# A linear-attention head whose seven levels are run on TensorE in two stretches in place of three

## The chip, the cores and the metric

One core of one Trainium2 chip runs the whole kernel. The metric is the device time in microseconds of one execution. A profiled execution leaves a trace, in which times are counted from the first instruction.

## The reference, cut to what matters

A decoder block of 16 sequences of 128 rows and 256 features: gated linear attention with 8 heads, then cross-attention, then a mixture of experts that takes 2 of 8. The change lies in the first part:

```python
q = l2norm(x @ Wq); k = l2norm(x @ Wk); v = x @ Wv; alpha = sigmoid(x @ Wg)   # per head: 128 wide
S_t = alpha_t[:, None] * S_{t-1} + k_t[:, None] * v_t[None, :]                 # scan over 128 steps
o_t = S_t.T @ q_t
out = concat_heads(o) @ Wo
```

## The kernel before

**Tiling.** The 16 sequences are 4 groups of 4. A group has 4 x 128 = 512 columns, and the unit of work is one head of one group: 32 units, counted n = 0 to 31, with h = n % 8 the head and i = n // 8 the group. Each engine has one list of instructions in an order written out by hand, and waits on counting semaphores. There is no loop on the chip.

**The levels.** The scan is replaced by a sum over pairs (s, t) of one sequence. A pair belongs to level l when s and t lie in neighbouring halves of a block of 2^(l+1) steps; s = t is the diagonal. For each level the operands q and k have to carry the product of the alphas from the middle of the block. So level l's operands are made from level l-1's: VectorE multiplies one half of them by spans of alpha (`decay(n, l)`, L646, for l = 6 L653), ScalarE copies the other half (`carry(n, l)`, L438), and neither may begin before both parts of level l-1 are there. Each level has one buffer, which unit n+1 may write only when TensorE has read it for unit n. TensorE multiplies the operands of a level in tiles of 32 x 32 (`block_products`, L1053, levels 0 to 4 and the diagonal; L1083, levels 5 and 6) into two banks, `lo_bank` and `hi_bank`. VectorE takes what a mask owns of the diagonal and levels 0 to 4 into `blocks` (`keep`, L677), six per unit. ScalarE spreads `blocks` over the diagonal of `attnT` (`expand_blocks`, L460) and copies levels 5 and 6 into it (`expand_wide`, L450 and L452).

**The order on TensorE** in iteration n: parts of the later layers at place "S", `project_v(n)` (L1043), alpha's projection for n+1 (L1030, `wg_sb`), the first run of levels, q's projection for n+1 (`wq_sb`), `attend_transposed(n-2)` (L1116), k's projection for n+2 (`wk_sb`), the second run of levels, `output_projection(n-2)` (L1128), parts at place "A", `attend(n-1)` (L1109), parts at "B", the third run of levels, and `norms(n)` (L1100). Results of projections go round a ring of four banks: a projection waits until the bank filled four fills before has been read.

**The order on ScalarE** in iteration n: `expand_wide(n-1)`, which waits for the last run of levels and for the norms of n-1; carries; `alpha_out(n+1)` (L403); `expand_blocks(n-1)`; `q_out(n+1)` (L410, L412); `oT_out(n-2)` (L465), for which `output_projection(n-2)` waits; `k_out(n+2)` (L419, L421); carries of n+1; copies for the later layers. Parts of the later layers stand before `alpha_out` ("early": `gelu` at h = 0, the exponentials of `probs_out` at h = 3, copies of `rowsT` at h = 5) and after `expand_blocks` ("mid": `gate_exp_out` at h = 6). When the function changes, a table is loaded.

**The order on VectorE** in iteration n: `norm_floor(n-1)` (L686), which waits for `expand_wide(n-1)`; the two keeps of `hi_bank` of n-1; decays; `v_scaled(n)` (L695), which frees the bank that k's projection takes; parts of later layers; `span_products(n+1)` (L663); `q_decayed(n+1)` (L704); the four keeps of `lo_bank` of n; decays of n+1; `o_scaled(n-1)` (L710).

Of the kernel before, what the change touches and what calls it, by code (L numbers as in the profile page):

```python
# [18 lines left out]
LEVELS = 7  # L19
BLOCK = 32  # L20
OUTER = LEVELS - 1
INNER = 5
# [15 lines left out]
def decoder_kernel(nc, x, ctx, ctxT, wq, wk, wv, wg, wo, xwT, gateT, expert, up_b,  # L38
# [7 lines left out]
    U = NG * H  # L46
# [5 lines left out]
    with ExitStack() as stack:  # L52
# [85 lines left out]
        lo_bank, hi_bank, acc0, acc1 = (bank(n) for n in ("lo_bank", "hi_bank", "acc0", "acc1"))  # L138
# [137 lines left out]
            return view(tensor, first, [[second - first, 2], [2 * w, N // (2 * w)], [1, w]])  # L276


        RUNS = ((0, 2), (1, 3, 4), (5, 6))
        DONE = {l: j + 1 for j, l in enumerate(l for run in RUNS for l in run)}  # L280
        LO_KEPT = 4

# [115 lines left out]
        def _(act):  # L398
# [24 lines left out]
            def carry(n, l):  # L423

                if n > 0:
                    act.wait_ge(level_mm, LEVELS * (n - 1) + DONE[l])
                if l == 1:
                    act.wait_ge(q0_set, n + 1)
                    act.wait_ge(k_set, n + 1)
                else:  # L430
                    act.wait_ge(decayed, OUTER * n + l - 1)
                    act.wait_ge(carry_set, OUTER * n + l - 1)
                if l < OUTER:
                    src, dst = (halves(n, m, 2 ** (l - 1), False) for m in (l - 1, l))
                else:
                    src, dst = (view(states, m * 2 * N + T // 2, [[N - BLOCK, 2], [T, GB], [1, BLOCK]])
                                for m in (l - 2, l - 1))
                nc.scalar.copy(dst, src).then_inc(carry_set, 1)  # L438

            def expand_wide(n):  # L440
                act.wait_ge(level_mm, LEVELS * (n + 1))
                act.wait_ge(norm_mm, min(n + 3, U + 1))
                positive(act, o_mm, n)
                near = hi_bank[:, AT_NEAR:AT_FAR].rearrange("p (b t) -> p b t", b=GB // 2)
                far = hi_bank[:, AT_FAR:AT_NORM].rearrange("p (b t) -> p b t", b=GB // 2)
                by_parity = attnT[:].rearrange("p (b m) t -> p b m t", m=2)
                for m in range(2):
                    for lo in (0, 2 * BLOCK):
                        at = lo + BLOCK * m
                        nc.scalar.copy(by_parity[lo:lo + BLOCK, :, m, lo + BLOCK:lo + 2 * BLOCK], near[at:at + BLOCK])  # L450
                    at = T // 2 * m
                    last = nc.scalar.copy(by_parity[0:T // 2, :, m, T // 2:T], far[at:at + T // 2])  # L452
                last.then_inc(near_out, 1)
# [83 lines left out]
            alpha_out(0)  # L537
            split_weights(3)
            q_out(0)
            for l in range(1, INNER):  # L540
                carry(0, l)
            for n in range(U):
                if n >= 1:
                    expand_wide(n - 1)
                carry(n, 5)
                carry(n, 6)
                tail_part(n, "early")
                if n + 1 < U:
                    alpha_out(n + 1)
                if n >= 1:  # L550
                    expand_blocks(n - 1)
                tail_part(n, "mid")
                if n + 1 < U:
                    q_out(n + 1)
                if n >= 2:
                    oT_out(n - 2)
                if n + 2 < U:
                    k_out(n + 2)
                if n + 1 < U:
                    for l in range(1, INNER):  # L560
                        carry(n + 1, l)
                tail_part(n, "end")
            expand_wide(U - 1)
# [39 lines left out]
        def _(dve):  # L603
# [60 lines left out]
                                            view(src, off + 1, [[2, m]]), ALU.mult).then_inc(span_set, 1)  # L664


            KEPT = ((lo_bank, 0, 0), (lo_bank, 1, 1), (lo_bank, 2, 3), (lo_bank, 3, 5), (hi_bank, 0, 2), (hi_bank, 1, 4))

            def keep(n, k):
                of_bank, at, mask = KEPT[k]  # L670
                positive(dve, kept, KEEPS * n + k)
                if k == 0:
                    dve.wait_ge(level_mm, LEVELS * n + INNER)
                    positive(dve, attnT_set, n)
                if k == LO_KEPT:
                    dve.wait_ge(near_out, n + 1)
                nc.vector.copy_predicated(blocks[:].rearrange("p b t -> p (b t)"), owned[:, mask].bitcast(U32),  # L677
                                          of_bank[:, N_IN * at:N_IN * at + N_IN]).then_inc(kept, 1)
# [211 lines left out]
            q_decayed(0)  # L890
            norm_floor(-1)
            dve.wait_ge(c_in, N_C)
            for l in range(1, INNER):
                decay(0, l)
            for n in range(U):
                if n >= 1:
                    norm_floor(n - 1)
                    for k in range(LO_KEPT, KEEPS):
                        keep(n - 1, k)
                decay(n, 5)  # L900
                decay(n, 6)
                v_scaled(n)
                tail_part(n, "early")
                if n + 1 < U:
                    span_products(n + 1)
                    q_decayed(n + 1)
                tail_part(n, "late")
                for k in range(LO_KEPT):
                    keep(n, k)
                if n + 1 < U:  # L910
                    for l in range(1, INNER):
                        decay(n + 1, l)
                tail_part(n, "mid")
                if n >= 1:
                    o_scaled(n - 1)
                if n == 0:
                    dve.wait_ge(w_in, N_W)
                tail_part(n, "end")
# [88 lines left out]
        def _(pe):  # L1007
# [49 lines left out]
            def levels(n, run):  # L1057

                if run == RUNS[0]:
                    pe.wait_ge(q_set, n + 1)  # L1060
                    pe.wait_ge(q0_set, n + 1)
                    pe.wait_ge(k_set, n + 1)
                    positive(pe, kept, KEEPS * (n - 1) + LO_KEPT)
                    block_products(lo_bank, 0, state0[:, 2 + n % 3], q_raw[:, n % 2])
                if run == RUNS[1]:
                    positive(pe, kept, KEEPS * n)
                    pe.wait_ge(norm_sq_set, n + 2)
                for l in run:
                    if l > 0:
                        pe.wait_ge(decayed, OUTER * n + l)  # L1070
                        pe.wait_ge(carry_set, OUTER * n + l)
                    tensor, at_q, at_k = state_at(n, l)
                    q, k = view(tensor, at_q, [[1, N]]), view(tensor, at_k, [[1, N]])
                    if l < INNER:
                        last = block_products(*((hi_bank, l // 2) if l % 2 else (lo_bank, 1 + l // 2)), k, q)
                    else:
                        w = 2 ** l
                        for b in range(GB):
                            m, col = b % 2, (AT_NEAR if l == INNER else AT_FAR) + w * (b // 2)
                            for s in (0, 2 * BLOCK) if l == INNER else (0, BLOCK):  # L1080
                                row = s + (BLOCK if l == INNER else 2 * BLOCK) * m
                                start = T * b + (s + w if l == INNER else w)
                                last = mm(hi_bank[row:row + BLOCK, col:col + w], k[:, T * b + s:T * b + s + BLOCK],  # L1083
                                          q[:, start:start + w], start=True, stop=True)
                    last.then_inc(level_mm, 1)
# [164 lines left out]
            for n in range(U + 1):  # L1250
                tail_part(n, "S")
                if n < U:
                    project_v(n)
                if n + 1 < U:
                    project(wg_sb, ("g", n + 1)).then_inc(g_mm, 1)
                if n < U:
                    levels(n, RUNS[0])
                if n + 1 < U:
                    project(wq_sb, ("q", n + 1)).then_inc(q_mm, 1)
                if n >= 2:  # L1260
                    attend_transposed(n - 2)
                if n + 2 < U:
                    project(wk_sb, ("k", n + 2)).then_inc(k_mm, 1)
                if n < U:
                    levels(n, RUNS[1])
                if n >= 2:
                    output_projection(n - 2)
                if n < U:
                    tail_part(n, "A")
                if n >= 1:  # L1270
                    attend(n - 1)
                tail_part(n, "B")
                if n < U:
                    levels(n, RUNS[2])
                if n + 1 < U:
                    norms(n)
            attend_transposed(U - 1)
# [84 lines left out]
```

## Time and profile before

| | |
|---|---|
| median of 3 runs | 564.17 us (562.89 to 567.42) |
| the profiled execution | 563.17 us, its span 561.4 us |
| granted clock of TensorE, mean | 0.951 of full speed |
| busy: TensorE, VectorE, ScalarE | 488.9, 383.1, 356.9 us |
| the 32 units | from 27.7 us to about 500 us of the span |

The span is the time from the first to the last instruction; 1.8 us of the profiled execution lie outside it. Busy times are sums over the instructions of an engine. The units repeat, so one unit can be read row by row and the others by how they differ from it.

### The profile page before, as it was taken

How to read it: one execution, taken by the hardware profiler on the slowest of the kernel's cores; microseconds unless marked ns; L12 is line 12 of the kernel's file. 1: busy time of each engine (PE TensorE's matmuls, PEld its weight loads, DVE VectorE, ACT ScalarE, POOL GpSimd, SP SyncE). 2: the span in 40 equal slices, each digit the busy share in tenths (PEclk: the TensorE clock that was granted, in tenths of full speed). 3: DMA queues.
4: the chain of work that ended last, by engine and by line, in shares of the span. 5: the costliest groups of instructions: out<-in, count | busy, mean ns of one | idle time of the engine just before them, and what ended most of it. 6: DMA issues, size and time to landing. Idle time of an engine off the chain costs nothing. (4 is left out here: it accounts for less than half of the span.)

```text
span 561.4 us, 25935 instructions
## 1 busy us (share of the span) xinstructions
PE 488.9 (87%) x11232; PEld 407.4 (73%) x11232; DVE 383.1 (68%) x1069; ACT 356.9 (64%) x825; POOL 85.1 (15%) x71
## 2 busy tenths in 40 slices
PE   1798999999988999899988999899988999775616
PEld 1587888888877888787867888688867887664415
DVE  4588887766786888765686887765775888614541
ACT  4667787766758677567758677577748676442202
POOL 1012111111111111410111111410111111300020
PEclk9999999999999999899999999899989999997557
DMA  8800000001010100210010100210000100201021
GB/s 334 252 3 5 4 4 4 4 4 40 4 41 2 41 4 4 77 41 22 23 40 5 40 4 4 78 40 22 23 2 4 40 5 4 78 0 39 0 75 37
DMA packets 15264, 20.35 MB, mean 36 GB/s; under 512 B 1200, under 2 KB 12976, under 8 KB 15152
## 3 DMA queue, kind: packets, MB, share of 16 engines
q1 hardware_dynamic: 13872, 14.49, 7.6%
q0 software_dynamic: 1280, 4.20, 2.6%
q8 instruction: 89, 1.46, 1.1%
q14 instruction: 23, 0.19, 0.1%
HBM read 16.60 MB, written 2.10 MB: 33 GB/s over the span
## 5 line engine op out<-in xcount | busy, mean ns | idle before, releaser
L438 ACT COPY states<-states 128x512 f32<-128x512 f32 (+1 forms) x160 | 94.6, 592 | 95.3 <-DVE states L646 88.6
L363 POOL TENSOR_TENSOR rnorm<-norm_sq,neg_half 128x8 f32<-128x8 f32 (+1 forms) x33 | 53.8, 1631 | 291.0 <-DVE norm_sq L686 291.0
L646 DVE TENSOR_TENSOR states<-states,spans 128x512 f32<-128x512 f32 x128 | 88.5, 691 | 12.2 <-DVE states L646 4.6
L1128 PE MATMUL acc<-wo_sb,oT_sb 128*128 128x256 f32 x256 | 63.8, 392 | 8.2 <-ACT oT_sb L465 8.2
L1030 PE MATMUL ring<-xnT,wk_sb 128*128 128x512 f32 x192 | 55.7, 429 | 8.9 <-DVE v_sb L695 6.0
L1043 PE MATMUL ring<-wv_sb,xnT 128*128 128x256 f32 x384 | 57.5, 302 | 0.6 <-DVE wv_sb L877 0.6
L1128 PEld LDWEIGHTS acc<-wo_sb,oT_sb 128*128 128x128 f32 x256 | 46.0, 189 | 15.3 <-ACT oT_sb L465 9.3
L1030 PE MATMUL ring<-xnT,wq_sb 128*128 128x512 f32 x192 | 53.1, 412 | 1.7 <-ACT rowsT L469 1.0
L677 DVE COPY_PREDICATED blocks<-owned,lo_bank 128x128 f32<-128x128 uint32 x128 | 38.5, 301 | 20.2 <-PE lo_bank L1053 14.8
L1043 PEld LDWEIGHTS ring<-wv_sb,xnT 128*128 128x128 f32 x384 | 50.9, 200 | 1.1 <-DVE wv_sb L877 0.7
L1030 PE MATMUL ring<-xnT,wg_sb 128*128 128x512 f32 x192 | 51.0, 402 | 0.0
L1030 PEld LDWEIGHTS ring<-xnT,wk_sb 128*128 128x128 f32 x192 | 36.1, 200 | 16.8 <-DVE v_sb L695 7.1
L1030 PEld LDWEIGHTS ring<-xnT,wq_sb 128*128 128x128 f32 x192 | 33.6, 188 | 9.2 <-ACT rowsT L469 1.4
L1030 PEld LDWEIGHTS ring<-xnT,wg_sb 128*128 128x128 f32 x192 | 35.0, 195 | 6.2 <-DVE xnT L749 0.2
L460 ACT COPY attnT<-blocks 32x128 f32<-32x128 f32 x128 | 37.4, 292 | 1.1
L1109 PEld LDWEIGHTS ring<-v_sb,attnT 128*128 128x128 f32 x256 | 33.0, 192 | 5.2 <-issue 4.3
L450 ACT COPY attnT<-hi_bank 32x64 f32<-32x64 f32 x128 | 26.0, 203 | 16.0 <-PE hi_bank L1100 8.5
L1109 PE MATMUL ring<-v_sb,attnT 128*128 128x128 f32 x256 | 33.8, 275 | 0.4 <-issue 0.4
L1100 PE MATMUL hi_bank<-ones,squares 128*32 128x1 f32 x2048 | 26.7, 173 | 7.8 <-issue 5.9
L1100 PEld LDWEIGHTS hi_bank<-ones,squares 128*32 128x32 f32 x2048 | 24.2, 110 | 10.1 <-issue 7.9
L663 DVE TENSOR_TENSOR spans<-spans 128x128 f32<-128x128 f32 (+3 forms) x128 | 28.4, 222 | 4.4
L1053 PE MATMUL lo_bank<-states 128*32 128x32 f32 x2048 | 29.6, 198 | 1.5 <-issue 1.5
(145 smaller groups left out, 852.4 us busy)
## 6 DMA issues: line engine op xcount, KB each, us to landing
x_buf<-x_dram SPq DMA_DIRECT2D x4, 512.0 KB, 4.2
ctxT_sb<-ctxT_dram SPq DMA_DIRECT2D x8, 256.0 KB, 3.4
ctx_sb<-ctx_dram SPq DMA_DIRECT2D x4, 512.0 KB, 4.8
out_dram<-x_mid SPq DMA_DIRECT2D x8, 256.0 KB, 2.1
states<-wk_dram SPq DMA_DIRECT2D x1, 1024.0 KB, 6.1
states<-wg_dram SPq DMA_DIRECT2D x1, 1024.0 KB, 8.1
states<-wq_dram SPq DMA_DIRECT2D x1, 1024.0 KB, 10.1
v_sb<-wv_dram SPq DMA_DIRECT2D x1, 1024.0 KB, 11.7
```

The source lines that it names most:

```text
L363: nc.gpsimd.tensor_tensor(rnorm[:, m % 4, first:last], norm_sq[:, first:last], neg_half[:, first:last], ALU.pow).then_inc(rnorm_set, 1)
L438: nc.scalar.copy(dst, src).then_inc(carry_set, 1)
L460: last = nc.scalar.copy(attnT[lo:lo + BLOCK, :, lo:lo + BLOCK], blocks[lo:lo + BLOCK])
L646: nc.vector.tensor_tensor(dst, src, by, ALU.mult).then_inc(decayed, 1)
L663: nc.vector.tensor_tensor(spans[:, span_at(l):span_at(l) + m], view(src, off, [[2, m]]), view(src, off + 1, [[2, m]]), ALU.mult).then_inc( ...
L677: nc.vector.copy_predicated(blocks[:].rearrange("p b t -> p (b t)"), owned[:, mask].bitcast(U32), of_bank[:, N_IN * at:N_IN * at + N_IN]). ...
L1030: last = mm(dst[:], w[:, a, c, P * h:P * h + P], xnT[:, i % 2, b, c], start=(c == 0 and k == 0), stop=(c == KC - 1 and k == 2))
L1043: last = mm(dst[:, 2 * P * k:2 * P * k + 2 * P], xnT[:, i % 2, a, c, T * b:T * b + T], wv_sb[:, w, c, 2 * P * pair:2 * P * pair + 2 * P], ...
L1053: last = mm(dst[BLOCK * r:BLOCK * r + BLOCK, to:to + BLOCK], left[:, at:at + BLOCK], right[:, at:at + BLOCK], start=True, stop=True)
L1100: last = mm(hi_bank[BLOCK * r:BLOCK * r + BLOCK, to:to + 1], squares[:, a, at:at + BLOCK], ones[:], start=True, stop=True)
L1109: last = mm(dst[:, P * b:P * b + P], attnT[:, b], v_sb[:, n // 2 % 2, b, n % 2], start=True, stop=True)
L1128: last = mm(accs[z][:, D * m:D * m + D], oT_sb[:, n % 2, T * b:T * b + T], wo_sb[:, h], start=(h == 0 and m == 0), stop=(h == H - 1 and m ...
```

## The change

Levels 1, 3 and 4 no longer have a run of their own between k's projection and the output projection. Level 1 joins the first run, levels 3 and 4 the last one. With that the banks are dealt anew: the diagonal and levels 0 to 2 lie in `lo_bank`, levels 3 to 6 and the norms in `hi_bank`, and the masks of the keeps follow. The four keeps of `lo_bank` wait for level 2 in place of level 4. The carries and decays of levels 3 and 4, whose buffers TensorE now frees only at the end of an iteration, move on ScalarE and VectorE from the end of iteration n to iteration n+1: behind `expand_wide` on ScalarE, in front of `v_scaled` on VectorE, while the decays of levels 5 and 6 go behind `v_scaled`. No instruction is added or taken away.

```diff
--- before.py
+++ after.py
@@ -276,7 +276,8 @@
             return view(tensor, first, [[second - first, 2], [2 * w, N // (2 * w)], [1, w]])
 
 
-        RUNS = ((0, 2), (1, 3, 4), (5, 6))
+        RUNS = ((0, 1, 2), (3, 4, 5, 6))
+        EARLY = 2
         DONE = {l: j + 1 for j, l in enumerate(l for run in RUNS for l in run)}
         LO_KEPT = 4
 
@@ -537,11 +538,13 @@
             alpha_out(0)
             split_weights(3)
             q_out(0)
-            for l in range(1, INNER):
+            for l in range(1, EARLY + 1):
                 carry(0, l)
             for n in range(U):
                 if n >= 1:
                     expand_wide(n - 1)
+                carry(n, 3)
+                carry(n, 4)
                 carry(n, 5)
                 carry(n, 6)
                 tail_part(n, "early")
@@ -557,7 +560,7 @@
                 if n + 2 < U:
                     k_out(n + 2)
                 if n + 1 < U:
-                    for l in range(1, INNER):
+                    for l in range(1, EARLY + 1):
                         carry(n + 1, l)
                 tail_part(n, "end")
             expand_wide(U - 1)
@@ -664,13 +667,13 @@
                                             view(src, off + 1, [[2, m]]), ALU.mult).then_inc(span_set, 1)
 
 
-            KEPT = ((lo_bank, 0, 0), (lo_bank, 1, 1), (lo_bank, 2, 3), (lo_bank, 3, 5), (hi_bank, 0, 2), (hi_bank, 1, 4))
+            KEPT = ((lo_bank, 0, 0), (lo_bank, 1, 1), (lo_bank, 2, 2), (lo_bank, 3, 3), (hi_bank, 0, 4), (hi_bank, 1, 5))
 
             def keep(n, k):
                 of_bank, at, mask = KEPT[k]
                 positive(dve, kept, KEEPS * n + k)
                 if k == 0:
-                    dve.wait_ge(level_mm, LEVELS * n + INNER)
+                    dve.wait_ge(level_mm, LEVELS * n + DONE[2])
                     positive(dve, attnT_set, n)
                 if k == LO_KEPT:
                     dve.wait_ge(near_out, n + 1)
@@ -890,16 +893,18 @@
             q_decayed(0)
             norm_floor(-1)
             dve.wait_ge(c_in, N_C)
-            for l in range(1, INNER):
+            for l in range(1, EARLY + 1):
                 decay(0, l)
             for n in range(U):
                 if n >= 1:
                     norm_floor(n - 1)
                     for k in range(LO_KEPT, KEEPS):
                         keep(n - 1, k)
+                decay(n, 3)
+                decay(n, 4)
+                v_scaled(n)
                 decay(n, 5)
                 decay(n, 6)
-                v_scaled(n)
                 tail_part(n, "early")
                 if n + 1 < U:
                     span_products(n + 1)
@@ -908,7 +913,7 @@
                 for k in range(LO_KEPT):
                     keep(n, k)
                 if n + 1 < U:
-                    for l in range(1, INNER):
+                    for l in range(1, EARLY + 1):
                         decay(n + 1, l)
                 tail_part(n, "mid")
                 if n >= 1:
@@ -1072,7 +1077,7 @@
                     tensor, at_q, at_k = state_at(n, l)
                     q, k = view(tensor, at_q, [[1, N]]), view(tensor, at_k, [[1, N]])
                     if l < INNER:
-                        last = block_products(*((hi_bank, l // 2) if l % 2 else (lo_bank, 1 + l // 2)), k, q)
+                        last = block_products(*((lo_bank, 1 + l) if l < 3 else (hi_bank, l - 3)), k, q)
                     else:
                         w = 2 ** l
                         for b in range(GB):
@@ -1261,8 +1266,6 @@
                     attend_transposed(n - 2)
                 if n + 2 < U:
                     project(wk_sb, ("k", n + 2)).then_inc(k_mm, 1)
-                if n < U:
-                    levels(n, RUNS[1])
                 if n >= 2:
                     output_projection(n - 2)
                 if n < U:
@@ -1271,7 +1274,7 @@
                     attend(n - 1)
                 tail_part(n, "B")
                 if n < U:
-                    levels(n, RUNS[2])
+                    levels(n, RUNS[1])
                 if n + 1 < U:
                     norms(n)
             attend_transposed(U - 1)
```

## Rows read from the trace of the kernel before

**Rows 1.** The page, busy time by engine, share of the span, instructions.

```profile
PE 488.9 (87%) x11232; PEld 407.4 (73%) x11232; DVE 383.1 (68%) x1069; ACT 356.9 (64%) x825; POOL 85.1 (15%) x71
```

**Rows 2.** Waits of all engines: total us, times, longest us.

```profile
PEld hi_bank L1053 <- issue: 11.7, 32, 0.6
...
PE acc L1128 <- ACT oT_sb L465: 8.2, 8, 2.9
...
PE ring L1030 <- DVE v_sb L695: 6.0, 3, 2.0
```

**Rows 3.** TensorE's timeline of unit 17 and first of 18: start, us, operation.

```profile
266.80 1.69 PE L1043 MATMUL ring<-wv_sb,xnT 128*128 128x256 f32 x12
...
270.42 0.46 PE L1053 MATMUL lo_bank<-states 128*32 128x32 f32 x32
270.80 1.66 PE L1030 MATMUL ring<-xnT,wq_sb 128*128 128x512 f32 x6
272.30 0.60 PE L1116 MATMUL ring<-ident,o_sb 128*128 128x128 f32 x4
272.66 1.65 PE L1030 MATMUL ring<-xnT,wk_sb 128*128 128x512 f32 x6
274.23 0.76 PE L1053 MATMUL hi_bank<-states 128*32 128x32 f32 x64
...
275.23 1.99 PE L1128 MATMUL acc<-wo_sb,oT_sb 128*128 128x256 f32 x8
...
279.17 1.69 PE L1043 MATMUL ring<-wv_sb,xnT 128*128 128x256 f32 x12
```

**Rows 4.** ScalarE's timeline of unit 17.

```profile
266.98 0.42 ACT L450 COPY attnT<-hi_bank 32x64 f32<-32x64 f32 x2 [3.48 <-PE hi_bank L1100]
...
268.28 0.62 ACT L438 COPY states<-states 128x512 f32<-128x512 f32 x1
269.88 0.41 ACT L438 COPY states<-states 128x256 f32<-128x256 f32 x1 [0.98 <-DVE states L646]
270.31 0.60 ACT L403 ACTIVATE alpha<-ring 128x512 f32<-128x512 f32 x1
270.81 1.21 ACT L460 COPY attnT<-blocks 32x128 f32<-32x128 f32 x4
272.50 0.59 ACT L410 COPY q_raw<-ring 128x512 f32<-128x512 f32 x1 [0.48 <-PE ring L1030]
...
273.48 0.59 ACT L465 COPY oT_sb<-ring 128x512 f32<-128x512 f32 x1
```

**Rows 5.** VectorE's timeline of unit 17, its decays and v.

```profile
269.12 0.68 DVE L646 TENSOR_TENSOR states<-states,spans 128x512 f32<-128x512 f32 x1
269.90 0.49 DVE L653 TENSOR_TENSOR states<-states,spans 128x128 f32<-128x128 f32 x2
270.31 0.68 DVE L695 TENSOR_TENSOR v_sb<-ring,rnorm 128x512 f32<-128x512 f32 x1
```

**Rows 6.** TensorE's timeline, output projection in unit 19.

```profile
306.93 2.00 PE L1128 MATMUL acc<-wo_sb,oT_sb 128*128 128x256 f32 x8 [0.92 <-ACT oT_sb L465]
```

**Rows 7.** Windows, units 18 to 24: length, busy PE PEld DVE ACT POOL, clock, DMA.

```profile
279.17:294.57 15.40, 13.43 (x353) 11.33 (x346) 13.55 (x39) 9.48 (x23) 2.69 (x2) 1.00 0.12 37
294.57:312.11 17.54, 15.51 (x373) 13.53 (x366) 12.86 (x40) 14.16 (x36) 2.69 (x2) 1.00 0.01 4
312.11:327.02 14.91, 14.34 (x353) 11.95 (x347) 13.52 (x42) 9.15 (x23) 2.75 (x2) 1.00 0.12 39
327.02:340.95 13.93, 13.51 (x354) 11.48 (x347) 11.03 (x27) 10.76 (x27) 1.64 (x1) 1.00 0.01 4
340.95:358.10 17.15, 15.38 (x349) 12.25 (x347) 13.73 (x55) 11.30 (x26) 6.12 (x5) 1.00 0.18 50
358.10:374.48 16.38, 16.38 (x355) 13.41 (x351) 10.21 (x24) 12.02 (x26) 1.67 (x1) 0.90 0.15 44
374.48:392.38 17.90, 17.60 (x378) 15.14 (x370) 10.25 (x24) 12.82 (x28) 1.64 (x1) 1.00 0.08 24
```

## The prediction

> **What bounds the kernel now.** I read the page's busy times first: TensorE is busy for 87% of the span, the others for 68% and less [rows 1]. Then the waits, for what takes the rest: inside the 32 units hardly anything but 8.2 us for `oT_sb` (8 times) and 6.0 us for `v_sb` (3 times) [rows 2]. So TensorE's own list sets the pace of a unit. Then the timelines of one plain unit, to see how far behind the other engines' chain of waits is. Unit 17 begins at B = 266.80 and unit 18 at 279.17: 12.37 us without a gap [rows 3]. ScalarE begins `expand_wide` at 266.98, B + 0.18, as early as it can, since it had waited [rows 4]. Its order then runs: carry 5, a wait of 0.98 us for VectorE, carry 6 at 269.88, alpha at 270.31, `expand_blocks`, q at 272.50, oT at 273.48, which ends at 274.07. The output projection that needs oT begins at 275.23. The cover is 1.16 us, and the bound in a plain unit is TensorE only for as long as that cover lasts. This is the number to watch.
>
> **The work on TensorE.** The same instructions remain. Run 2 takes 274.23 to 275.23, 1.00 us for three levels; the last level of run 1 takes 270.42 to 270.80, 0.38 us [rows 3]. So level 1 in the first run costs 0.36 and levels 3 and 4 in the last one 0.64, together the 1.00 that goes. What remains is the entry into a run: from k's projection to the tiles is 1.57 us (272.66 to 274.23), from q's to the full transposes 1.50 us (270.80 to 272.30) [rows 3]. I take 0.07 us a unit, 2.2 us in all. The weight path shows more at that entry: 11.7 us of idle, 32 times, 0.37 us each [rows 2]; the matmuls cover most of it, so 0.37 is the upper bound. Entering the longer runs elsewhere is no new cost, as those runs were there. The Trainium skill ("TensorE: Matmul & The Clock Gate", The mechanism) says that a weight load overlaps matmuls in flight only where their row groups differ, so that tiles cannot be loaded ahead behind a full-array matmul. The idle weight path at the entry fits that; it would make a removed entry worth the whole 0.37, the first rival below.
>
> **When TensorE wants oT.** Before at B + 8.43 (275.23 less 266.80). Now 1.00 and 0.07 go from in front of it and 0.36 comes in: B + 7.72, which is 0.71 earlier.
>
> **When ScalarE has oT.** Carries 3 and 4 now stand between `expand_wide` and carry 5, and each waits for VectorE's part of the level below. Counted from E, the start of `expand_wide`, with unit 17's durations [rows 4, 5]: carry 3 starts at E + 1.30 (268.28 less 266.98). VectorE starts its first decay at E + 2.14, behind the norms and two keeps as before, and ends it at 2.82. Carry 4 follows at 2.90. Decay 4 starts 0.78 behind decay 3, as decay 6 behind decay 5 now, at 2.92, and ends at 3.60. Carry 5 starts at 3.68. But decay 5 stands behind `v_scaled`, which begins near 3.5 and takes 0.68 less some overlap, so decay 5 runs from 4.16 to 4.84. Carry 6 starts at E + 4.90, where before it was 2.90 (269.88). ScalarE is 2.0 us later. From carry 6 the rest has no more room: 0.43 to alpha, 0.50 to `expand_blocks`, 1.21 to q, whose own result is ready by then, so that the 0.48 us of waiting there goes, 0.98 to oT, 0.59 for oT. That is E + 8.61, B + 8.79. In unit 19, where oT is late already, the output projection starts at 306.93 [rows 6]; I add 0.05 for the step over the semaphore: B + 8.84. Bounds on the delay: 1.4 if `v_scaled` were to cost the chain nothing, 2.2 if each handshake costs 0.1 more.
>
> TensorE wants it at 7.72. It waits for 1.12 us, with attention, the last levels and the norms queued behind that wait, and the next `expand_wide` behind these. So nothing catches it up. The remainder of the unit was 3.94 (275.23 to 279.17) and is 4.58 with 0.64 of levels 3 and 4. A plain unit takes 8.84 + 4.58 = 13.42, against 12.37: 1.05 more. I take 1.0, since other plain units lag by some tenths at their start now, which the emptier end of ScalarE's iteration takes away. Plain are units 2 to 8, 9, 17 and 25: 10 of them, **+10.0**.
>
> **The other units**, from unit 18 to 24's windows, in which length less busy time is the wait [rows 7]. The heads repeat for three groups.
> - h = 2 (18): 15.40 long, 1.97 idle for `v_sb`. VectorE enters this unit late, behind the residual and the norm's statistics. Now it keeps `lo_bank` without waiting for a second run, and has two decays of 0.68 fewer in front of them, so that wait goes. 13.42 and the transposes of x2T (15.40 less 1.97 less 12.37, 1.06) make 14.5: -0.9, three times **-2.8**.
> - h = 3 (19): 17.54 long, 2.03 idle, of which 0.92 is for oT [rows 6]. It starts at B + 12.36. The exponentials stand in the same chain, where the table load covers part of the 2.0; I take the start as B + 12.95, less the late start of ScalarE that goes. With 0.64 behind: +1.2, **+3.7**.
> - h = 4 (20): 14.91 long, 0.57 idle. Cross-attention in front of v gives ScalarE some 2 us. No wait for oT; the 0.5 at the start goes: **-1.6**.
> - h = 5 (21): 13.93 long. Copies of `rowsT` stand behind carry 6, and q's projection waits for their bank (0.42 now). That wait grows by the 2.0 less what the transposes in front cover: +1.5, **+4.6**.
> - h = 6 (22): a table load and `gate_exp` stand in the chain, 1.4 us. oT at B + 8.8 + 1.4 = 10.2, against 8.9 now (8.43 and some 0.5 for the gate's matmuls in front, an estimate), and 0.64: +2.0 twice, and +2.5 in unit 30, which has no k projection in front: **+6.5**.
> - h = 7 (23, clock 0.90): a table load of 1.3 stands before alpha. The slow clock covers it in part: +0.8 twice; unit 31 has neither g nor q nor k in front, +2.0: **+3.6**.
> - h = 0 with experts (24): 0.30 idle, all of it for oT. ScalarE is 2.0 later, 0.64 behind it: +2.65 twice, **+5.3**.
>
> The sum is 10.0 - 2.8 + 3.7 - 1.6 + 4.6 + 6.5 + 3.6 + 5.3 = 29.3 us. On the profiled execution's 563.17 that is 592.5 (1.8 of them outside the span). The median of the runs is 1.0 above that execution, inside their spread, so I leave **592.5 us**.
>
> **The rivals.**
> - *TensorE keeps its pace.* The point from which it decides: the cover of 1.16 less the 0.71 by which TensorE is earlier, 0.45 us. If ScalarE's chain grows by less, oT never stalls, and what moved is hidden. For it: TensorE has no gap in unit 17, and ScalarE's last carries were late at the end of an iteration before. Against it: the two carries stand in front of alpha in an ordered queue, and growing by 2.0 is four times the limit. It gives 2.2 for the entries, 5.9 for the waits for `v_sb` [rows 2] and 1.6 for h = 4: 563.2 - 9.7 = 553.5. With an entry worth 0.37, 11.7 in place of 2.2, it is 544. Without either relief, 561. By the skill's rule on row groups it would be the 544.
> - *Half of it.* Only the units in which oT is late already, or has a table load in its chain, lose, and the plain ones fit: the above less the plain ones' 10.0 is 582; with the lower bound of the chain (1.4 in place of 2.0 in some 27 units, 16 us less) 576.
> - *The clock.* Unit 23 shows a mean granted clock of 0.90, so part of it ran at the lower of the two levels, 1.2 GHz [rows 7]. The new waits of over 3 us at h = 0 and h = 3 and of over 2 us at h = 6 might bring more such stretches. Unit 23 has no wait and would last some 14.6 at full speed (a plain unit, keys and the transposes, an estimate), so one costs 1.5 to 2; six of them 9 to 12: 601 to 604.
>
> **How the numbers follow.** My forecast, a stall of about 1 us in each unit, has 0.65, with its own range of 583 to 600. Half of it 0.16, the clock 0.08, TensorE keeps its pace 0.11. What leaves out no more than 2 in 10 is 572 to 602: the forecast, most of the half case and some of the clock. One per cent, 5.6 us, is about what a measurement tells from no change. Faster by more than that takes the rival with its reliefs: 0.07. Within it: that rival without the reliefs, or both effects small: 0.06. Slower 0.87.
>
> **What would show it.** In the trace after: waits of the output projection for `oT_sb` in some 25 units in place of 8, and 30 us in place of 8; plain units 13.4 us long; carry 6 4.9 us behind the start of `expand_wide`, ScalarE waiting 2 us at the end of an iteration for the norms; no more waits for `v_sb`; the run of levels 3 to 6 without a wait in front. If plain units last 12.3 us with oT on time, the step "when ScalarE has oT" is wrong. It would be wrong too if VectorE's chain were faster than its rows, or if `expand_wide` could start before B.

## The result

The changed kernel takes 612.85 us (median of 4 runs, 609.35 to 613.44) against 563.53 us: a ratio of 1.085 (95% interval 1.078 to 1.092). The profiled execution has a span of 610.8 us, 49.4 more than before. Of all executions below one (of e1, 575.87 us) was in a slower state of the chip; the ratios leave it out, the median of e1 has it in.

The page of the changed kernel, busy times and the granted clock of TensorE by slices:

```profile
PE 504.7 (83%) x11232; PEld 419.1 (69%) x11232; DVE 380.4 (62%) x1069; ACT 358.9 (59%) x825; POOL 83.5 (14%) x71
...
PEclk9999899999989999999998999998989998788656
```

Against [rows 1]: TensorE executes the same 11232 matmuls but is busy for 15.8 us more, and the rest of its span has grown from 72.5 us (561.4 less 488.9) to 106.1 (610.8 less 504.7), 33.6 us more. Together these are the 49.4. A busy time that grows with the same instructions is the clock: the mean granted clock fell from 0.951 to 0.927. In windows of 1 us the lower level appears in 4 stretches (13.6 us in all) before the last unit begins in the kernel before, and in 11 (35.5 us) in the changed one.

The waits of TensorE in the changed kernel: total us, times, longest. They answer to [rows 2], and the last line is one more of the kernel before.

```profile
PE acc L1133 <- ACT oT_sb L466: 35.2, 22, 3.2
...
PE hi_bank L1105 <- issue: 6.5, 4, 2.2
...
PE ring L1048 <- issue: 4.2, 4, 1.3
PE ring L1035 <- issue: 3.2, 4, 1.7
PE hi_bank L1058 <- issue: 3.1, 8, 0.5
...
PE lo_bank L1058 <- issue: 2.2, 3, 0.8
```

```profile
PE hi_bank L1100 <- issue: 5.9, 13, 0.5
```

Waits for oT went from 8.2 us to 35.2. TensorE's waits for `v_sb` (6.0) have no row any more. Waits on issue, in which TensorE waits for nothing that the profile shows, grew from 12.7 us to 20.7. They are not new: the last line, of the kernel before, is as large as the one for `v_sb`, and I passed over it.

Two kinds are mixed in them. In units 14, 22 and 30 TensorE stops several times in a row for 0.2 to 0.5 us, always while the rows of the experts' weights are being fetched (a transfer of some 6 us, 227.9 to 233.8 us in unit 14 of the kernel before). These come to 5.1 us before, 3.1 in the changed kernel, 5.1 in e5, 3.1 in e6 and 5.4 in e7 below, and to nothing in the other runs, which fetch the same rows. What ties them to the transfer is not shown. The rest is 7.5 us before and 17.5 in the changed kernel; the long stops in it are of the kind that unit 2 shows below.

TensorE's timeline of the plain unit 5, to be laid beside [rows 3]:

```profile
94.56 1.69 PE L1048 MATMUL ring<-wv_sb,xnT 128*128 128x256 f32 x12
...
98.17 0.75 PE L1058 MATMUL lo_bank<-states 128*32 128x32 f32 x64
...
100.70 1.65 PE L1035 MATMUL ring<-xnT,wk_sb 128*128 128x512 f32 x6
103.37 1.99 PE L1133 MATMUL acc<-wo_sb,oT_sb 128*128 128x256 f32 x8 [1.03 <-ACT oT_sb L466]
...
106.19 0.77 PE L1058 MATMUL hi_bank<-states 128*32 128x32 f32 x64
...
107.19 0.76 PE L1105 MATMUL hi_bank<-ones,squares 128*32 128x1 f32 x64
107.89 1.70 PE L1048 MATMUL ring<-wv_sb,xnT 128*128 128x256 f32 x12
```

Its unit is 13.33 us long (94.56 to 107.89). The output projection starts at B + 8.81 with 1.03 us of waiting. ScalarE in the same unit, beside [rows 4]:

```profile
94.74 0.42 ACT L451 COPY attnT<-hi_bank 32x64 f32<-32x64 f32 x2 [2.62 <-PE hi_bank L1105]
...
96.03 0.62 ACT L439 COPY states<-states 128x512 f32<-128x512 f32 x1
97.63 0.62 ACT L439 COPY states<-states 128x512 f32<-128x512 f32 x1 [0.97 <-DVE states L649]
98.41 0.62 ACT L439 COPY states<-states 128x512 f32<-128x512 f32 x1 [0.16 <-DVE states L649]
99.61 0.41 ACT L439 COPY states<-states 128x256 f32<-128x256 f32 x1 [0.58 <-DVE states L649]
100.04 0.60 ACT L404 ACTIVATE alpha<-ring 128x512 f32<-128x512 f32 x1
...
101.76 0.58 ACT L411 COPY q_raw<-ring 128x512 f32<-128x512 f32 x1
...
102.73 0.59 ACT L466 COPY oT_sb<-ring 128x512 f32<-128x512 f32 x1
```

`expand_wide` begins at E = 94.74, carry 3 at E + 1.29, carry 4 at 2.89, carry 5 at 3.67, carry 6 at 4.87, alpha at 5.30, oT at 7.99 and ends at 8.58. Carries 4, 5 and 6 each wait for VectorE.

The second loss stands in unit 2, the same work, 15.68 us long. TensorE's timeline:

```profile
59.22 2.00 PE L1133 MATMUL acc<-wo_sb,oT_sb 128*128 128x256 f32 x8 [1.01 <-ACT oT_sb L466]
...
62.04 0.76 PE L1058 MATMUL hi_bank<-states 128*32 128x32 f32 x64
...
63.05 0.68 PE L1105 MATMUL hi_bank<-ones,squares 128*32 128x1 f32 x54
65.90 0.26 PE L1105 MATMUL hi_bank<-ones,squares 128*32 128x1 f32 x10 [2.17 <-issue]
66.09 2.81 PE L1048 MATMUL ring<-wv_sb,xnT 128*128 128x256 f32 x12
68.70 1.99 PE L1035 MATMUL ring<-xnT,wg_sb 128*128 128x512 f32 x6
```

After 54 of the 64 matmuls of the norms TensorE stands for 2.17 us, though nothing releases it, and then goes on with the other 10. The transfers of 60 to 68 us in 40 slices of 0.2 us:

```profile
GB/s 0 0 0 0 0 0 0 0 0 0 0 0 0 0 0 0 82 0 0 0 0 0 0 0 0 0 0 0 0 0 0 0 0 0 0 0 0 0 0 82
...
q8 instruction: 2, 0.03, 1.9%
```

There is nothing but two packets of instructions of 16 KB. The first lies in the 17th slice, 63.2 to 63.4 us; TensorE, which has just taken 300 short instructions since 62.04 (150 matmuls and their weight loads), stops at about 63.7 and goes on at 65.90. Behind it the clock falls; the window from 64 to 70 us (length, busy PE PEld DVE ACT POOL, clock, DMA share, GB/s):

```profile
64.00:70.00 6.00, 4.10 (x26) 3.85 (x26) 2.83 (x13) 2.54 (x9) 2.64 (x2) 0.72 0.01 3
```

v and g's projection (66.09 to 70.62) take 4.53 us in place of 3.00 in unit 5.

The other stops look alike. Besides the rows of short stops there are 13 of 0.6 us or more within the units of the changed kernel. In 12 of them TensorE goes on 2.2 to 2.9 us after a packet of instructions has started (in one after 4.0). Count TensorE's matmuls and weight loads from the start: the stops stand at numbers 1447, 2201, 3207, 4965, 5217, 6975, 10485, 12743, 13993, 14745, 14997, 18511 and 21017. Each distance is a whole number of times 250 to 252, and 252 is the mean of a packet (22464 in 89 packets). That fits stops at the borders of packets; the profile shows how large packets are, but not which instructions are in one.

### The profile page after: what moved, and what is told of

The parts are those of the page before. It is cut to its first block and busy times, and to the rows that moved or that the text cites. A ratio compares the mean times of both kernels' runs of the same rounds, so it can differ in the third digit from the quotient of the medians.

```text
span 610.8 us, 25935 instructions
## 1 busy us (share of the span) xinstructions
PE 504.7 (83%) x11232; PEld 419.1 (69%) x11232; DVE 380.4 (62%) x1069; ACT 358.9 (59%) x825; POOL 83.5 (14%) x71
## 5 line engine op out<-in xcount | busy, mean ns | idle before, releaser
L1133 PE MATMUL acc<-wo_sb,oT_sb 128*128 128x256 f32 x256 | 71.3, 427 | 35.4 <-ACT oT_sb L466 35.2
L1133 PEld LDWEIGHTS acc<-wo_sb,oT_sb 128*128 128x128 f32 x256 | 50.8, 208 | 53.5 <-ACT oT_sb L466 46.6
L1048 PE MATMUL ring<-wv_sb,xnT 128*128 128x256 f32 x384 | 59.2, 307 | 4.8 <-issue 4.2
L1048 PEld LDWEIGHTS ring<-wv_sb,xnT 128*128 128x128 f32 x384 | 52.2, 204 | 5.7 <-issue 4.5
L689 DVE TENSOR_SCALAR norm_sq<-hi_bank 128x8 f32<-128x8 f32 (+1 forms) x33 | 5.5, 166 | 61.2 <-ACT attnT L453 44.0
L713 DVE TENSOR_TENSOR o_sb<-ring,rnorm 128x512 f32<-128x512 f32 x32 | 22.1, 690 | 33.4 <-PE ring L1114 33.2
L666 DVE TENSOR_TENSOR spans<-alpha 128x256 f32<-128x256 f32 x32 | 13.6, 424 | 37.0 <-ACT alpha L404 36.9
```

Source lines behind the costliest of these rows:

```text
L713: nc.vector.tensor_tensor(o_sb[:], ring_of(("o", n))[:].rearrange("p (b v) -> p b v", b=GB), rnorm[:, (n - 1) % 4, 0:GB].unsqueeze(2).broa ...
L1048: last = mm(dst[:, 2 * P * k:2 * P * k + 2 * P], xnT[:, i % 2, a, c, T * b:T * b + T], wv_sb[:, w, c, 2 * P * pair:2 * P * pair + 2 * P], ...
L1133: last = mm(accs[z][:, D * m:D * m + D], oT_sb[:, n % 2, T * b:T * b + T], wo_sb[:, h], start=(h == 0 and m == 0), stop=(h == H - 1 and m ...
```

## The experiments

I tested two theories. S: all of it is ScalarE's chain in front of oT, and the clock follows from its waits. F: the longer run of small tiles (levels 3 to 6 and the norms, 320 instructions in some 2 us) also outruns the supply of instructions. Each ratio is to the kernel before on the same chip. "Low clock" is the time at the lower level up to the last unit's start, from windows of 1 us.

| | ratio (95%) | TensorE busy, rest of span | oT | issue | low clock |
|---|---|---|---|---|---|
| before | 1 | 488.9, 72.5 | 8.2 | 12.7 | 13.6 |
| changed | 1.085 (1.078 to 1.092) | 504.7, 106.1 | 35.2 | 20.7 | 35.5 |
| e1 | 1.021 (1.013 to 1.029) | 494.1, 75.9 | 16.2 | 13.9 | 23.9 |
| e3 | 1.042 (1.040 to 1.044) | 488.5, 86.3 | 30.1 | 5.5 | 10.2 |
| e5 | 0.981 (0.977 to 0.985) | 485.9, 65.7 | 10.2 | 9.8 | 6.8 |

All columns but the ratio are of one execution each. From one execution of e1 to the next the mean granted clock went from 0.934 to 0.952, and one stretch at the lower level (3.4 us) is worth 0.003 of it (an estimate: half of 3.4 in 570). So a difference of a few stretches between two kernels says little.

**e1, carries 5 and 6 behind oT.** Two runs on TensorE as in the changed kernel.

```diff
 (ScalarE)                                   (VectorE)
   carry(n, 3); carry(n, 4)                    decay(n, 3); decay(n, 4); v_scaled(n); decay(n, 5)
-  carry(n, 5); carry(n, 6)                  - decay(n, 6)
   ... alpha_out, expand_blocks, q_out         ... span_products(n + 1), q_decayed(n + 1)
   oT_out(n - 2)                               keep(n, 0..3)
+  carry(n, 5); carry(n, 6)                  + decay(n, 6)
```

(The spans of level 5, which decay 6 reads, get a second place for odd n.)

> The changed kernel, with carries 5 and 6 moved on ScalarE from in front of alpha to behind oT (VectorE's decay 6 follows the four keeps). Theory S (ScalarE's chain in front of oT is the whole cause; the lower clock follows from its waits): the output projection stands at B + 7.7 to 7.9 in a plain unit, waits for oT fall from 35 us to under 8, low-clock stretches inside the units from 12 to about 4, time 556 to 568 us. Theory F (the longer run of small tiles, levels 3 to 6 and the norms, outruns the supply of instructions to TensorE): the waits for oT go as well, but TensorE's idle time put down to issue stays near 19 us, as do half of the low-clock stretches, time 575 to 590 us.

Measured 572.78 us, ratio 1.021 (1.013 to 1.029), between the two ranges. The waits in question:

```profile
PE acc L1134 <- ACT oT_sb L466: 16.2, 12, 3.2
...
PE hi_bank L1106 <- issue: 5.2, 6, 1.9
...
PE ring L1049 <- issue: 3.7, 3, 1.6
```

Plain units without a stop are 12.15 us long (5, 8, 17), 0.2 to 0.3 less than before, and their output projection stands at B + 7.65. So the theory on ScalarE's chain holds where it speaks, and the timing on TensorE's side (7.72) too. But units 2, 3, 7 and 9 are 14.2, 14.7, 15.4 and 14.1 us long (unit 3 has no stop of its own: the clock is low in it from 63.3 us on, behind that of unit 2), and the row of unit 2 is the one from above, at the same instruction:

```profile
62.49 0.26 PE L1106 MATMUL hi_bank<-ones,squares 128*32 128x1 f32 x10 [1.89 <-issue]
```

The numbers 2201, 6975, 10485, 13993, 18511 and 21017 are places of stops in e1, e2 and e4 as well. oT fell only to 16.2, as it stays late in the units with exponentials (B + 10.2) or experts.

**e2, two runs, carries and decays where they stood before.**

```diff
-        EARLY = 2
+        EARLY = 4
-   carry(n, 3..6)                                (ScalarE)
+   carry(n, 5); carry(n, 6)
-   decay(n, 3); decay(n, 4); v_scaled(n); decay(n, 5); decay(n, 6)
+   decay(n, 5); decay(n, 6); v_scaled(n)         (VectorE)
```

> Two runs on TensorE and the new banks as in the changed kernel, but all carries and decays stand where they stood before (levels 1 to 4 at the end of an iteration, where those of levels 3 and 4 now wait for the last run to have read their buffers). Theory S: oT comes at about B + 6.9, no waits for it in plain units, but the wait at the iteration's end makes VectorE late with v in units after residual and statistics: 558 to 572 us. Theory F: the same with 10 to 20 us more, from issue idle near 19 us and the low-clock stretches behind it: 575 to 590 us.

Measured 581.22 us, ratio 1.038 (1.032 to 1.044): oT 13.8 us, issue 22.1 us, low clock 34.1 us, as theory F had it. A second way to take the new carries away from in front of oT leaves the same stops, and units 2, 3, 7 and 9 as long (14.2, 14.7, 16.0 and 14.2 us).

**e3, levels 3 and 4 in a run of their own.** ScalarE and VectorE as changed.

```diff
-        RUNS = ((0, 1, 2), (3, 4, 5, 6))
+        RUNS = ((0, 1, 2), (3, 4), (5, 6))
+   levels(n, RUNS[1])          # (3, 4), between k's projection and
    output_projection(n - 2)
```

> The changed kernel, in which TensorE takes levels 3 and 4 in a run of their own between k's projection and the output projection; ScalarE and VectorE as in the changed kernel. Theory S: oT still comes at B + 8.8, but TensorE does 0.66 us of the work while it waits: plain units 12.7 us, 16 to 20 us less than the changed kernel's 613, so 592 to 597. Theory F: the run in front of v is short again, so that the issue idle falls from 19 us to about 11 and with it low-clock stretches: 578 to 590 us.

Measured 580.29 us, the waits:

```profile
PE acc L1133 <- ACT oT_sb L466: 30.1, 25, 2.9
...
PE hi_bank L1058 <- issue: 2.7, 1, 2.7
```

Plain units are 12.68 us, as both theories had it; their output projection is at B + 8.82 as before the edit, so the chain on ScalarE is untouched. But issue idle is 5.5 us (1.5 of it in the units), the low clock 10.2 us, and units 2, 3, 7 and 9 lose their extra (12.8, 13.6, 14.4, 12.7). The gain over the changed kernel is 4.3 points. The waits for oT are 0.25 to 0.45 us in plain units here and up to 2.7 elsewhere. Nine of those in the units are of 1.8 us or more; right behind two of them (2.02 us before 294.1, 1.85 before 393.0) the clock falls, and behind the other seven it doesn't.

**e4, v behind all decays.**

```diff
-                v_scaled(n)
                 decay(n, 5)
                 decay(n, 6)
+                v_scaled(n)
```

> The changed kernel with v_scaled moved on VectorE behind the decays of levels 5 and 6; nothing else. Theory S: carry 6 starts 0.65 us earlier behind the start of expand_wide (4.25 in place of 4.9), plain units shrink from 13.33 to 12.7 us, waits for oT from 35 to about 20 us, and with fewer low-clock stretches 588 to 598 us. Theory F: the waits for oT shrink as well but issue idle stays near 19 us with its low clock: 598 to 603 us.

Measured 596.05 us, ratio 1.070 (1.063 to 1.078). Plain units are 12.95 us (13.33 changed), a gain of 0.4 and not 0.65; oT 30.2, issue 18.8, low clock 17.1 us. The issue idle stays, as theory F had it. VectorE's order in front of carry 6 has its price, but is the smaller part of what a plain unit lost.

**e5, both cures: e1's edit and e3's together.** Banks and the first run as in the changed kernel.

> Both cures together: carries 5 and 6 behind oT as in e1, and levels 3 and 4 in a run of their own in front of the output projection as in e3; diagonal and levels 0 to 2 still in the first run, banks as in the changed kernel. If the 49 us are these two causes (S and F) and the low clock that follows their idle: waits for oT about 14 us as in e1 (heads with exponentials or experts), issue idle about 6 us as in e3, no waits for v, low-clock stretches in the units 3 to 5, time 548 to 560 us, same as before or faster. If the new banks or the longer first run carry a cost of their own, 565 us or more.

Measured 554.56 us, faster than the kernel before. The page's first line and TensorE's, and its waits:

```profile
span 551.6 us, 25935 instructions
...
PE 485.9 (88%) x11232; PEld 406.5 (74%) x11232; DVE 376.2 (68%) x1069; ACT 353.7 (64%) x825; POOL 84.1 (15%) x71
```

```profile
PE acc L1134 <- ACT oT_sb L466: 10.2, 8, 2.9
...
PE hi_bank L1106 <- issue: 5.1, 11, 0.5
```

No unit waits for v, and nothing remains of the 49 us. With e1, e3 and the changed kernel it makes a square: two runs in place of three cost 4.0 points with late carries (e1 against e5) and 4.3 with carries in front (changed against e3); carries in front cost 6.1 points with three runs (e3 against e5) and 6.4 with two (changed against e1). So the two causes add up, to within the intervals of about a point. e5 also shows that the new share of the banks and the longer first run cost nothing.

**e6, 128 instructions more at the start.** The changed kernel with 32 more calls, which the profile has as 64 matmuls and 64 weight loads:

```diff
             pe.wait_ge(ident_in, 16)
+            for _ in range(32):
+                mm(lo_bank[:, 0:BLOCK], ident[:], ident[:, 0:BLOCK], start=True, stop=True)
```

> The changed kernel with 32 extra small matmuls at the start of TensorE's list (128 instructions of it), where it waits for the first input anyway; nothing in the units changes. Theory F (instructions come in packets of a fixed count, and a packet is late when its border falls into the run of small tiles): the idle put down to issue moves to other units than 2, 3, 7 and 9 (15.68, 14.64, 16.29 and 15.58 us long in the changed kernel), which shrink to 13.4 to 14.5, while others grow; the time stays within 600 to 620 us. Theory S, or any cause that lies in the units' own work: the same units stay long.

Measured 621.28 us, ratio 1.097 (1.092 to 1.102), a little above the range. The first unit starts 7.7 us later (35.03 against 27.31), since the new matmuls hold TensorE from 5.03 to 18.89 us, and its next work started at 9.70 without them; from there to the last unit's start it takes 499.3 us, against 498.1. Within that the lengths moved: unit 2 from 15.68 to 14.35, 7 from 16.29 to 15.07, 9 from 15.58 to 14.32, 11 from 20.28 to 18.88, while 4 grew from 13.83 to 15.30, 12 from 13.62 to 15.99, 26 from 18.28 to 20.23 and 27 from 17.81 to 20.44. Unit 3 hardly changed (14.65 to 14.22). The stops stand on the same grid of numbers, with the 128 new instructions counted in: at 3711, 6727, 7229 and 9233, again 250 to 252 or a multiple apart, and at 12745, where the changed kernel has one at 12743, but 128 instructions earlier in the work. Work that is identical in each unit stalls by its place in TensorE's list: this is the supply of instructions, not the work. Unit 7 came down less than expected.

**e7, attention between levels 3 and 4 and levels 5 and 6.** As e1, but the last run is short.

```diff
+   levels(n, RUNS[1])          # (3, 4)
    attend(n - 1)
    tail_part(n, "B")
-   levels(n, RUNS[1])          # (3, 4, 5, 6)
+   levels(n, RUNS[2])          # (5, 6)
```

> As e1 (572.8 us, issue idle 13.9), but attention and the later layers' parts at place B stand between levels 3 and 4 and levels 5 and 6, so that the last run is again as short as before and the output projection starts as early as in e1. Theory F: the issue idle falls to 5 to 8 us and the low-clock stretches in the units from 8 to 3 to 5, time 553 to 562 us. If not the length of the run of small tiles but their place at the end of the unit matters: 570 to 575 us as e1.

Measured 576.59 us, ratio 1.018 (1.013 to 1.023), no better than e1: issue 14.5, low clock 20.1 us. Theory F had 553 to 562 us, so as I had written it, by the length of one run, it is wrong. Half of it came true: 5.4 of the 14.5 us are stops during the experts' fetches, which e1 has none of, so the other kind fell from 13.9 us to 9.1. The stop stands at the same instruction still, only shorter:

```profile
62.31 0.26 PE L1106 MATMUL hi_bank<-ones,squares 128*32 128x1 f32 x10 [1.05 <-issue]
```

Attention takes 1.0 us for 16 instructions (8 matmuls), so from levels 3 and 4 to the norms there are as many as before, and 16 more, in 3 us in place of 2. In e5 the output projection lies between as well, 1.8 us for another 16, and the stops in units 2, 3, 7 and 9 are gone. So an unbroken run is not needed; a count over some 3 us fits these runs, where the 3 us are my estimate. The stops of unit 2 also show what sets their length. TensorE goes on 2.4 us after the packet's start in e1 and 2.6 in e7, but 178 instructions remained to be taken at that start in e7 and 63 in e1. Why that packet starts so late is open.

**e8, the same results with fewer instructions.** As e1, with the norms by whole columns of weights:

```diff
-  for r in range(T // BLOCK):
-      mm(hi_bank[BLOCK * r:BLOCK * r + BLOCK, to:to + 1], squares[:, a, at:at + BLOCK], ones[:])
+  mm(hi_bank[:, to:to + 1], squares[:, a, T * b:T * b + T], ones[:])
```

> As e1 (572.8 us, issue idle 13.9 us, last run in one piece), but the norms are taken with 8 matmuls over all 128 rows in place of 32 over 32 rows, so that the burst behind attention has 224 instructions in place of 320; results are the same. Theory F, in the form that the count of instructions within some 3 us matters: issue idle falls to 6 us or less, and units 2, 3, 7 and 9 lose their extra 1.5 to 2 us, while each unit gains 0.3 to 1.2 us for wider weight loads; time 572 to 600 us. If issue idle stays at 13 us, the count is not the cause.

Measured 601.78 us, ratio 1.081 (1.077 to 1.086). The page:

```profile
span 605.4 us, 22863 instructions
...
PE 539.9 (89%) x9696; PEld 461.2 (76%) x9696; DVE 375.5 (62%) x1069; ACT 354.9 (59%) x825; POOL 84.5 (14%) x71
```

Issue idle fell from 13.9 us to 2.0 with the last run in one piece and at the same place, as theory F had it. Together with e6 that leaves the supply of instructions as the cause of the stops. e8 doesn't part the count from the pace, since the norms take longer too, and packets are divided elsewhere. The time is another matter, a little above the range: the norms take 1.81 us a unit in place of 0.7, and the low clock rose to 51.2 us in 12 stretches, though TensorE waits less than in e1. I had left the clock out of this expectation, and idle time alone doesn't explain it.

**e9, the kernel before with e1's move alone.**

> The kernel before with only the move of e1: carries 5 and 6 behind oT on ScalarE, decay 6 behind the four keeps on VectorE; three runs, levels and banks as before. If what e5 gained (554.6 us, 0.981 of before) comes from the order on ScalarE and VectorE: waits for oT 8 to 6 us and for v gone or nearly, 551 to 558 us, the same as e5. If the new share of the levels (0, 1, 2 in the first run) is what gained: 0.99 to 1.0 of before.

Measured 562.33 us, ratio 1.011 (1.007 to 1.015). oT 7.0, and v still 7.3 us in three units. So the order on ScalarE alone gains nothing before; e5's gain needs the new share as well. In it VectorE keeps the tiles of `lo_bank` without waiting for a second run and does two decays fewer at the end of an iteration; that this is what frees `v_sb` fits the waits, but no run tests it alone.

## Why the prediction was right in direction and wrong in size

**TensorE's work and when it wants oT: right.** B + 7.72 was forecast; e1, where oT ends at B + 7.56, shows 7.65. What one entry is worth is read best from e1 against e5, which has one run more and the same order on the other engines: 12.14 to 12.17 us against 12.27 to 12.32, so some 0.14 a plain unit, between my 0.07 and the 0.37 of the weight path. The whole 0.37 of the first rival is not seen.

**When ScalarE has oT: right.** Carry 6 at E + 4.90 was forecast and 4.87 measured, oT at E + 8.61 and 8.58, the output projection at B + 8.84 and 8.81, the plain unit 13.42 and 13.33. Waits for oT: 30 us in some 25 units forecast, 35.2 in 22 measured. The wait of ScalarE for the norms at the end of an iteration is 2.2 to 2.6 us, where 2 was forecast.

**The relief for v: right.** The waits of 6.0 us are gone. But the next unit takes part of that back: units 10 and 11 together went from 35.57 to 36.74 us, 18 and 19 from 35.45 to 38.41, 26 and 27 from 35.33 to 36.09, 4.9 us in all where the sum had -2.8 + 3.7 = 0.9.

**The other terms**, from v to v, so that what stands at S counts for the unit before. h = 5: +4.6 forecast, 4.4 measured. h = 6: 6.5 and 7.95. h = 7 (without unit 31): 1.6 and 0.9. h = 0 with experts: 5.3 and 6.7. h = 4: -1.6 and +1.1. Units 0 and 1, which the sum left out: +1.0. Plain units: 10.0 and 16.4. In units 4, 5, 6, 8, 17 and 25 it is 0.9 to 1.3 each as forecast (unit 4 gets there by a stop of 0.77 us and not by waiting for oT); units 2, 3, 7 and 9 bring 10.0 where the sum had 4.0.

**The step that failed** is in "The work on TensorE": "The same instructions remain" and "Entering the longer runs elsewhere is no new cost". It counted the time of the instructions and not their density, and the forecast took their clock as given. Both terms stood at nothing. TensorE from the first unit's v to the last one's, in us:

| | length | busy | wait for oT | for v | issue |
|---|---|---|---|---|---|
| before | 454.8 | 431.9 | 4.6 | 6.0 | 9.9 |
| changed | 498.1 | 443.5 | 29.6 | 0 | 19.3 |
| e3 | 464.0 | 429.0 | 26.5 | 0 | 1.5 |

The stretch grew by 43.3 us, where the sum had 27.3 (29.3 less the 2.0 of unit 31). What it had priced, the waits for oT and v, brings 25.0 - 6.0 = 19.0, and other waits 3.3. Issue brings 9.4 and the same instructions at a lower clock 11.6: these 21 us have no term in it, and the supply of instructions was no rival of mine either. The reading in "What bounds the kernel now" had already passed over the 9.9 us of issue in the units, more than the 6.0 for v.

e3 takes both away. From e3 to the changed kernel the stretch grows by 34.1 us: 17.8 of issue, 14.5 of busy time, 3.1 of waits for oT, and 1.3 less of others. The 0.64 us of moved levels are in there too, but not as a sum of their own: a plain unit pays 0.65 for them (13.33 against 12.68), a unit with h = 4 at most 0.14, and where a stop or the low clock comes first, the wait for oT behind it is shorter or gone.

e3 also tests the price of the queue on ScalarE. Plain units agree: 2.9 us over the kernel before, where the sum without the moved levels has 3.6. All units together don't. In the sum the 0.64 stand in the 21 units that wait for oT, 13.4 us, so 14 of the 27.3 should be left, and e3 has 9.2. The largest difference is at h = 6: 4.6 us were expected for the three units and 3.0 were gained, as e3 doesn't have the 5.1 us of stops during the experts' fetches.

The rest of the miss lies behind the last unit's v: 85.4 us against 78.9, where I had 2.0 more; the granted clock is 0.83 in the changed kernel's first 35 us there and 0.92 in the same stretch of the kernel before.

The ratio of e3 (1.042) is larger than its trace has it (574.8 against 561.4, 1.024): the kernel before took between 556 and 565 us at the median on the chips of these runs, and each trace is one execution. So the ratios rank the kernels, and the traces say where time lies.

**The clock** was a rival with 0.08, priced at 9 to 12 us for six stretches. It came along with the forecast, with 7 stretches more up to the last unit. That it was written as an alternative and not as a companion of the forecast was the second mistake. Of the ten stretches behind the first unit of the changed kernel four begin 1 to 3 us after the start of a stop of 1.3 to 2.2 us (units 2, 9, 26, 29). Five begin 2 to 3.4 us after the start of a wait for oT of 2.0 to 2.5 us, at h = 0, 3 and 6 as the rival had it, and one behind short stops during a fetch. So the clock follows both causes. But 2 of the 5 waits of 2.54 us have nothing behind them, and e8 has nearly no stops and 51.2 us of low clock, part of it with no wait in front. What in the activity decides is open.

The range ended at 602, since I had set the forecast and the clock side by side where they had to be added: that alone gives 601 to 604, and the stops come on top.

## What to carry to other kernels

Before merging runs of small matmuls, count TensorE's instructions over a few microseconds, not their time: the same instructions closer together can wait for their own supply, and longer instructions in between hide that. Where a buffer is freed later, follow every step that moves behind it through the queue that it now stands in; the chain from `expand_wide` to oT could be summed to 0.03 us from rows of one unit. What loses by the queue can win by a reorder of the same queue: e5 keeps the new banks and the longer first run, though three runs, and is 1.9% faster than the kernel before.

## What the hardware showed that I had not expected

Instructions reach TensorE in packets of 16 KB: 89 packets for the whole kernel, and 22464 matmuls and weight loads, about 250 a packet. In unit 2 a packet goes at 63.2 us and TensorE resumes at 65.90, 2.7 us later. A plain unit needs 676 of them in 13.3 us, 51 a microsecond, and its dense stretch 320 in some 2 us, 160 a microsecond. The Trainium skill ("Runtime: NRT & Kernel Launch", Instruction fetch mechanics) gives the same 16 KiB blocks of 256 instructions, and says that crossing a border is mostly hidden. Here it isn't always: without the short stops during the fetches, issue idle is 17.5 us in the changed kernel, 5.5 in e3 and 2.0 in e8, and the long stops lie a whole number of packets apart.

The granted clock took its two levels only, 1.2 and 2.4 GHz. In unit 2 it fell behind a stop of 2.17 us, and in the kernel before behind one of the three waits of about 2 us for v (at 413 us) and twice behind short stops during the experts' fetches; waits of 1.0 us in plain units brought none.
